# A scan stage in which ScalarE makes state 8's decays ahead of the silus, and two neighbouring orders of work change with it

## The reference

```
raw, gate = split(x @ W_in)
h  = silu(conv(raw) + conv_b)                    # 4 taps, causal
ts, Bmat, C = split(h @ W_x)
dt = softplus(ts @ W_dt + b_dt)
dA = exp(dt[..., None] * A);  dBu = dt[..., None] * Bmat[:, :, None, :] * h[..., None]
state = dA * state + dBu;     y = einsum('bhd,bd->bh', state, C)     # scan over the tokens
out = ((y + h * D) * silu(gate)) @ W_out
```

## Time and profile before

| | us |
|---|---|
| median of 3 runs | 1278.0 |
| the three runs | 1276.61 to 1281.53 |
| the profiled execution | 1280.58 |
| its span, first to last instruction | 1278.8 |
| VectorE busy over the span | 955.2 |
| TensorE, ScalarE, GpSimd busy over the span | 1082.7, 748.4, 730.6 |

### The profile page before, as it was taken

One profiled execution on the slowest core, in us unless ns is written; L12 is line 12 of the kernel. 1 busy time (PEld: TensorE's weight loads), 2 busy tenths in 40 slices (PEclk: granted clock), 3 DMA queues, 4 the chain that ended last, 5 costly groups with the idle time before them and its releaser, 6 DMA issues. The chain is left out here.

```text
span 1278.8 us, 16507 instructions
## 1 busy us (share of the span) xinstructions
PE 1082.7 (85%) x4934; PEld 547.4 (43%) x4934; DVE 955.2 (75%) x1181; ACT 748.4 (59%) x1306; POOL 730.6 (57%) x640
## 2 busy tenths in 40 slices
PE   7876799999999987888989898989898388887853
PEld 3322244444444433333334333333335277776753
DVE  4898585665755439999999999999991876565545
ACT  6586545655556255767767686857653345454445
POOL 0222261431513005899898989897983167777764
PEclk8898899999999998999999999999998589999986
DMA  7000000000000003222322222222210111111225
GB/s 232 1 0 0 1 1 1 1 1 1 1 1 1 1 0 109 100 83 93 98 84 88 86 84 92 70 69 77 73 58 9 58 36 50 51 54 51 50 58 182
DMA packets 33966, 67.21 MB, mean 53 GB/s; under 512 B 7168, under 2 KB 7360, under 8 KB 33664
## 3 DMA queue, kind: packets, MB, share of 16 engines
q1 hardware_dynamic: 28464, 55.23, 13.4%
q0 software_dynamic: 4992, 10.23, 3.0%
q10 hardware_dynamic: 432, 0.76, 0.2%
HBM read 56.63 MB, written 9.57 MB: 52 GB/s over the span
## 5 line engine op out<-in xcount | busy, mean ns | idle before, releaser
L1936 POOL TENSOR_TENSOR prod<-hs,csb 128x1024 f32<-128x1024 f32 x128 | 301.9, 2359 | 125.3 <-DVE hs L1982 120.0
L1982 DVE TENSOR_TENSOR_SCAN hs<-dA,first,pD 128x1024 f32<-128x1024 f32 x128 | 300.4, 2347 | 5.2 <-DVE pD L1995 0.8
L1664 PE MATMUL pY<-prod,const 128*128 128x512 f32 x512 | 241.5, 597 | 5.0 <-POOL prod L1936 5.0
L1809 ACT ACTIVATE dA<-dt,negA 128x511 f32<-128x511 f32 x256 | 169.4, 712 | 1.5 <-DVE dt L2037 1.4
L1995 DVE TENSOR_TENSOR pD<-dtu,pD 128x1024 f32<-128x1024 f32 x128 | 154.9, 1211 | 10.0 <-ACT pD L1824 9.7
L1664 PEld LDWEIGHTS pY<-prod,const 128*128 128x128 f32 x512 | 97.5, 192 | 109.9 <-issue 92.2
L2471 POOL DMA_INDIRECT g<-moe_rows,source x78 | 82.4, 1056 | 55.5 <-DVE source L2666 26.7
L2717 DVE SCALAR_TENSOR_TENSOR hid<-pR,silu 128x512 f32<-128x512 f32 x78 | 53.9, 692 | 67.2 <-ACT silu L2425 67.2
L1162 ACT ACTIVATE stage<-pR,vec 128x512 f32<-128x512 f32 x64 | 43.9, 687 | 99.7 <-PE pR L891 99.5
L2490 POOL DMA_INDIRECT moe_outs<-y,to x78 | 81.1, 1039 | 26.2 <-issue 22.8
L1824 ACT ACTIVATE pD<-first 128x1 f32<-128x1 f32 x128 | 21.6, 169 | 119.4 <-PE pD L1674 98.2
(11 more groups left out here) (477 smaller groups left out, 2588.1 us busy)
## 6 DMA issues: line engine op xcount, KB each, us to landing
csb<-ssm_c SPq DMA_DIRECT2D x128, 256.0 KB, 3.1
raw<-moe_w SPq DMA_DIRECT2D x12, 512.0 KB, 4.8
room<-moe_outs SPq DMA_DIRECT2D x8, 512.0 KB, 8.3
hidw<-hid_w SPq DMA_DIRECT2D x1, 2048.0 KB, 10.0
moe_rows<-xt SPq DMA_DIRECT2D x8, 256.0 KB, 2.0
outT<-X SPq DMA_DIRECT2D x8, 256.0 KB, 2.0
X<-xT SPq DMA_DIRECT2D x3, 512.0 KB, 4.1
g<-moe_rows,source POOLq DMA_INDIRECT x78, 2.6
```

The source lines that it names most:

```text
L1664: last = nc.tensor.matmul(YB[c][:], G.ident, prod[:, slot(b, n), c, :], start=n == 0, stop=n == DST - 1)
L1809: last = nc.scalar.activation(dA[:, slot(b, n), c, 1:N], dt[:, b, c, 1:N], ACT.Exp, scale=negA[:, c, n:n + 1])
L1936: nc.gpsimd.tensor_tensor(prod[:, slot(b, n), :, :], hs[:, slot(b, n), :, :], csb[:, slot(b, n), :, :].to_broadcast([P, CB, N]), ALU.mult)\
L1982: nc.vector.tensor_tensor_scan(hs[:, slot(b, n), :, :].rearrange("p c n -> p (c n)"), dA[:, slot(b, n), :, :].rearrange("p c n -> p (c n)" ...
```

## The change

In state 2 TensorE now spreads state 3 ahead of the convolution's first passes. ScalarE makes the decays of states 7 and 8 one after the other in state 6, then loads the silu table by a line of its own, then splices state 7, does the silus and loads the other table back; in state 7 only the splice of state 8 is left. The last body, which prepares no other, splices state 7 right after the decays. The weights are split in states 1 and 3 instead of 2 and 7. GpSimd makes dt times h, and with it the first token, right behind the sum of dt, both in state 12.

```
@@ TensorE, body
+                    if n == 2:
+                        spread_B(t, b, n + 1)
                     if not is_last(t, b) and n in PE_PREP:
                         prep(*after(t, b), PE_PREP.index(n))
-                    if n + 1 < DST:
+                    if n != 2 and n + 1 < DST:
                         spread_B(t, b, n + 1)
@@ ScalarE, prep
                 elif step == 4:
+                    act.preload_act_table_set("silu_and_others")
+                    splice(*before(t, b), 7)
                     act.wait_ge(S["parked"], chunk(t, b, CB - 1))
                     nc.scalar.activation(h[b][:, :, :], h[b][:, :, :], ACT.Silu).then_inc(S["h"], 1)
@@ ScalarE, body
-                    if n + 1 < DST:
+                    if n == 6:
+                        decay(t, b, 7)
+                        decay(t, b, 8)
+                        if is_last(t, b):
+                            splice(t, b, 7)
+                    elif n == 7:
+                        splice(t, b, 8)
+                    elif n + 1 < DST:
                         decay(t, b, n + 1)
                         splice(t, b, n + 1)
...
-                    if splits(t) and n in (2, 7):
-                        split_weights(t, b, (2, 7).index(n))
+                    if splits(t) and n in (1, 3):
+                        split_weights(t, b, (1, 3).index(n))
@@ GpSimd, body
-                    if not is_last(t, b) and n in (8, 11, 12, 13):
-                        prep(*after(t, b), (8, 11, 12, 13).index(n))
+                    if not is_last(t, b) and n in (8, 11, 12):
+                        prep(*after(t, b), (8, 11, 12).index(n))
+                    if not is_last(t, b) and n == 12:
+                        prep(*after(t, b), 3)
```

## The result

| | before | after |
|---|---|---|
| median of 10 runs | 1280.61 us | 1285.66 us |
| the runs | 1276.61 to 1281.68 us | 1283.48 to 1288.0 us |
| profiled execution | 1280.58 us | 1283.57 us |
| its span | 1278.8 us | 1281.7 us |

The ratio after to before is 1.0047, 95% interval [1.0033, 1.0061]: slower by about 6 us. The forecast was 1270.7, and the time lies above the range. It lies near the time, 1284.7, that the prediction gave to its slower rival, which had a chance of 0.07.

The account below looks back on a forecast made before the run. VectorE was taken to bound the scan stage, its gain lying in waits for ScalarE's splice. 1.57 + 1.5 + 3.9 + 0.31 = 7.3 us off 1278.0 gave 1270.7 us; range 1266.0 to 1277.5.

Parts of the forecast that it names:

- slower rival: TensorE's clock falls at sum 13, state 1 waits 2.5 us, 2.0 lost in each of seven bodies: 1284.7; chance 0.07.
- the GpSimd part: GpSimd's two products together: first token earlier, state 0's 0.31 us wait in body 2 goes, product 13 runs later.
- I cost this at nothing: TensorE's 2.3 us wait ahead of sum 13 costs nothing: VectorE's multiply is 0.3 us ahead, another 1.05 in the copy.
- The copy as a cushion: VectorE's three-column copy waits out GpSimd's product 0, so it can give back 1.05 us of a delay at state 1.
- State 8, bodies 2, 3, 5, 7 (1.57): VectorE's waits for ScalarE's splice at state 8, 0.40 + 3 x 0.39 us, go in full.
- Body 1 (1.5): Of waits of 0.99 + 2.36 us at states 3 and 8, 1.8 won, 0.3 taken back at state 11.
- the wait near 1 at state 7: A sign of the forecast being right: in body 1 VectorE waits near 1 us for the splice at state 7.
- Bodies 4 and 6 (3.9): Waits at states 4 and 8, 3.96 us together, nearly all go, with TensorE's clock kept up at the convolution.
- The lower bound, 1.8 of 3.96: Gain in bodies 4 and 6 if TensorE's clock falls at the convolution as before, taken from body 1's 1.5 of 3.35.
- Spread 3, the splits: Spread 3 ahead of the convolution costs nothing and frees states 3 and 4; the moved weight splits cost nothing.
- State 0 (0.31): VectorE's 0.31 us wait for the first token at state 0 of body 2 goes; body 4's 0.21 is worth nothing.
- The two rivals of the middle: Wait moves to state 7: 1274.3, chance 0.13. GpSimd sets the pace, its copy retaking gains: 1275.8, chance 0.12.

Follow-up runs that it names:

- e2: Kernel before with only GpSimd's two dt products put together: 1290.57 us against 1279.06, ratio 1.0088.
- e6: Changed kernel with the copy of three columns of xn made by ScalarE instead of VectorE: 1269.59 us against 1280.05, ratio 0.9922.
- e3: Changed kernel with eight idle matmuls of 512 columns in TensorE's wait ahead of sum 13: 1271.17 us against 1279.06, ratio 0.9924.
- e5: Changed kernel with TensorE's spread 1 ahead of sum 13: 1275.76 us against 1280.05, ratio 0.9975.
- e1: Changed kernel with GpSimd's two dt products apart again, as before the change: 1269.57 us against 1279.06, ratio 0.9922.
- e4: Kernel before with only ScalarE's change to states 7 and 8 (both decays in state 6, early silu load): 1271.26 us against 1279.06, ratio 0.9940.
- e9: Changed kernel with eight idle matmuls ahead of sum 13 and the copy of xn on ScalarE: 1264.55 us against 1280.40, ratio 0.9873.
- e11: Kernel before with only the copy of three columns of xn on ScalarE: 1268.64 us against 1280.40, ratio 0.9909.
- e8: Kernel before with only spread 3 ahead of the convolution: 1275.97 us against 1280.05, ratio 0.9967.

## Why the prediction was wrong, point by point

**The step that failed** is the last of the GpSimd part, "I cost this at nothing", for the wait of TensorE ahead of sum 13, with the 0.07 that followed from it. The wait was foreseen in place and length (2.3 us; 2.07 to 2.93 measured). Three things in it were wrong.
- The clock. From 2 falls in 5 waits of 2.07 the prediction took a fall to be an exception. It fell in 7 of 7 in the profiled execution of the kernel after, in 5 of 7 in e2 and in 3 of 7 in e6. The fall is the main cause: e3 keeps product 13 late and the clock up, and most of the loss is gone; in e2 the two bodies with the clock up lose less than half a microsecond each.
- The copy as a cushion. The prediction counted on 1.05 us that the copy would give back. It looked at the copy's end only, not at what VectorE has to have before it starts: the root, which hangs on sum 13 through the centring and the Square (e5). A late root carried the copy past the end of product 0 into product 1, and instead of giving back 1.05 it took 1.3 more: 2.03 a copy instead of 0.72.
- The wait for the root itself, 2.8 us, was in no sum.

**The slower rival** named place and cause, and its 1284.7 is 1 us from the measured time. That it is so close is partly luck: it took the pair's loss as 14 us and the gains as 7.3, and the runs show some 16 (1.0047 against e1's 0.9922) and 10. Its price was made up otherwise, too. State 1 waits 0.65 to 1.39 instead of 2.5, in six bodies and not in seven: the clock fell only during sum 13, whose four passes took 2.44 to 2.97 us where body 1's passes at the lower level took 3.78. The rest came from root and copy, which was to give time back.

**State 8, bodies 2, 3, 5, 7 (1.57)**: right; the waits are gone after, in e1 and in e4.

**Body 1 (1.5)**: about right at the clock that the working took as given, and too small where the clock was up earlier. The profiled executions show body 1 with a lower and a higher clock, both with and without the edit: 0.53 before, 0.57 in e5 and 0.55 in e9, but 0.75 in e2 and 0.78 in e11, whose body 1 is as in the kernel before, and 0.75 in e1 (means over 7 us around the convolution's first passes). Unchanged, states 3 and 8 wait 0.99 + 2.36 at the lower clock and 0.37 + 1.31 in e2; e11 shows 3.40 us for passes that took 3.78 before:

```profile
491.19 3.40 PE L1593 MATMUL pQ<-xn,convw 128*128 128x512 f32 x4 [3.60 <-DVE xn L1969]
```

With the change and the lower clock the wait near 1 at state 7 that the prediction named is there, 0.92 in e5 and 0.93 in e9:

```profile
506.13 1.23 DVE L2010 TENSOR_TENSOR pD<-dtu,pD 128x1024 f32<-128x1024 f32 x1 [0.92 <-ACT pD L1830]
```

State 8 starts 30.1 us after state 0 in e5 and 30.2 in e9, where it was 32.2 before: some 2.0 won, where 1.8 was expected ahead of state 11. With the higher clock, as in e1 and in the kernel after, no wait is left at states 3 to 8: in e1 state 8 starts 28.8 us after state 0 (512.51 less 483.73), 3.4 less than before. Of these 3.4 us about half comes with the clock of that execution and not with the change: in e2, unchanged there, it is 30.5.

**Bodies 4 and 6 (3.9)**: right in sum. The reason given, that spread 3 divides the wait and may spare the fall, isn't borne out: in e4, without spread 3, the waits at state 8 are gone as well; in e8, with it, the clock falls elsewhere; and with it, it fell after waits of 1.35 (e1, body 6), 0.84 and 1.36 (e8, bodies 5 and 7), all shorter than the 2.07 of the kernel before. What covers a fallen clock is ScalarE's early decay and load: where it fell, in body 6, 0.56 is left in e4 and 0.27 in e1 of the 1.98 before. The lower bound, 1.8 of 3.96 with the clock down, was too low.

**Spread 3, the splits**: the splits cost and win nothing (0.9999). Spread 3 alone wins 0.33%; beside ScalarE's part (e4 0.9940, e1 0.9922, intervals overlapping) its share can't be told.

**State 0 (0.31)**: the wait is gone after, and is 0.28 in e1, where the pair is apart. It is all that the pair wins.

**The sum without the pair**: 7.0 was forecast for it, and e1 measures 0.9922 of 1279.06, 10 us; its interval runs from 6.9 to 13.2. **The two rivals of the middle**: in the kernel after no wait moved to state 7; in e1 and e3 only 0.27 and 0.22 did, in one body each. GpSimd's pace came true only in so far as the copy waits for it.

What stays open: why waits of 2 to 2.5 us at the same place let the clock fall in some bodies and executions and not in others (in e8 and e11, with the products apart, it fell at sum 13 of body 2 after 1.94 and 1.93 us, in the kernel before it stayed up there after 1.93), what sets body 1's clock, and why e5's runs fall into 1273 to 1278 and 1281 to 1284.

## What to carry to other kernels

Before an operation is moved ahead of another on one engine, ask who waits for the one that is now later, and whether that engine's wait lets its clock fall: a wait of 2 us that costs nothing by itself can nearly double the price of the work behind it (the centring took 1.92 us instead of 1.02). Where a slack is to absorb a delay, follow every input of the instruction in which the slack lies, for a late input can turn it from cover into loss. When a change has several parts, time each alone: here one part won 0.6%, one 0.3%, one nothing, and one lost 0.9%. And before a gain seen in one profile is put down to an edit, look at whether the clock was the same there: a stretch that the edit doesn't touch can tell.

## What the runs showed of the hardware that was not expected

A copy of 128 x 3 values on VectorE took from 0.14 us, with GpSimd between products, to 2.38 us (e3), and where it was long it ended with the product that GpSimd had running (613.96 against 613.94). The multiply (with PSUM on both sides) and the scan (with PSUM as one input) kept 1.20 to 1.23 and 2.35 us throughout.

TensorE's granted clock fell after all seven waits of 2.07 to 2.93 us in the kernel after (0.80 to 0.81 over 8 to 9 us, 0.50 over 3.4 us of body 3), but only after five of seven in e2 and three of seven in e6. Eight idle matmuls in the wait, which left 0.35 to 1.20 us of it, kept it at 1.00 in all seven, in e3 and again in e9.
